# Two MLP-and-pooling layers on one core: the first pair of hidden tiles reordered by tiles of x, its weights and their halves sent and used in another order

## What is computed

```python
h = gelu(x @ fc1_w.T + fc1_b)                 # 512 -> 2048, exact gelu
y = concat(h @ fc2_w.T + fc2_b,               # 2048 -> 384, shared
           h @ experts_w[tok].T + experts_b[tok])   # 2048 -> 128, one expert per sequence
x = x + y
s = tanh(x @ W1 + b1) @ v                     # one score per row
p = softmax(where(mask[type], s[None, :], -1e30))   # per row: prefix, suffix or all but itself
x = x + (p @ x) / mask.sum(-1)
```

## Time and profile before

| | |
|---|---|
| median of 3 runs | 784.71 us (783.61 to 785.57) |
| the profiled execution | 784.57 us |
| its span | 782.8 us |
| TensorE busy | 770.2 us, 98% of the span, 3462 matmuls |
| VectorE busy | 402.5 us, 51% |
| ScalarE busy | 387.0 us, 49% |
| GpSimd busy | 132.7 us, 17% |

### The profile page before, as it was taken

How to read it: one execution, slowest core, us unless ns; L and a number is a source line. 1 busy time by engine, 2 the same in 40 slices (tenths; PEclk the granted TensorE clock), 3 DMA queues, 4 the chain that set the end, 5 groups by cost and what they waited for, 6 DMA issues and landing times.

```text
span 782.8 us, 11478 instructions
## 1 busy us (share of the span) xinstructions
PE 770.2 (98%) x3462; PEld 626.9 (80%) x3462; DVE 402.5 (51%) x713; ACT 387.0 (49%) x665; POOL 132.7 (17%) x184
## 2 busy tenths in 40 slices
PE   9999999999999999999999999999999999999977
PEld 6788888888888888888888888888887888888865
DVE  6854667563445332754536433376245542255666
ACT  6856665443546433543546633446254653344552
POOL 3172221400011121410001022050001102114011
PEclk9999999999999999999999999999999999999998
DMA  6899998877854568867776466985787466787722
GB/s 215 281 346 330 307 338 271 268 228 231 236 190 149 175 204 280 259 202 239 225 228 188 147 209 216 284 253 178 232 252 219 144 194 207 223 284 208 228 67 108
DMA packets 130715, 176.93 MB, mean 226 GB/s; under 512 B 10064, under 2 KB 97632, under 8 KB 130656
## 3 DMA queue, kind: packets, MB, share of 16 engines
q1 hardware_dynamic: 130496, 176.20, 72.0%
q0 software_dynamic: 160, 0.01, 0.0%
HBM read 136.33 MB, written 39.85 MB: 225 GB/s over the span
## 4 chain that ended last, share of the span: by engine, by line
PE 95%; DVE 2%; ACT 1%; DMA 1%; issue 0%; SPq 0%; DVEq 0%; ACTq 0%
PE y L765 15%; PE y L767 15%; PE y L766 15%; PE hA L765 8%; PE hA L767 7%; PE hA L766 7%; PE hF L765 6%; PE hF L766 6%; PE hF L767 5%; PE j L858 2%; PE j L765 1%; PE j L767 1%; PE j L766 1%; PE j L866 1%; PE j L835 1%; PE j L834 1%
## 5 line engine op out<-in xcount | busy, mean ns | idle before, releaser
L765 PE MATMUL y<-hs,w2c 128*128 128x512 f32 x512 | 201.8, 394 | 0.2
L767 PE MATMUL y<-hs,w2c 128*128 128x512 f32 x512 | 199.6, 390 | 0.0
L766 PE MATMUL y<-hs,w2c 128*128 128x512 f32 x512 | 199.4, 389 | 0.0
L765 PEld LDWEIGHTS y<-hs,w2c 128*128 128x128 f32 x512 | 96.1, 188 | 22.1 <-DVE hs L1263 1.9
L767 PEld LDWEIGHTS y<-hs,w2c 128*128 128x128 f32 x512 | 96.1, 188 | 20.5
L766 PEld LDWEIGHTS y<-hs,w2c 128*128 128x128 f32 x512 | 96.2, 188 | 19.3
L765 PE MATMUL hA<-xch,w1c 128*128 128x512 f32 x252 | 100.0, 397 | 0.9 <-DVE xcl L1263 0.6
L767 PE MATMUL hA<-xch,w1c 128*128 128x512 f32 x252 | 98.6, 391 | 0.0
L766 PE MATMUL hA<-xcl,w1c 128*128 128x512 f32 x252 | 98.6, 391 | 0.0
L1035 ACT ACTIVATE hst<-hst,bcol 128x512 f32<-128x512 f32 x62 | 43.9, 721 | 85.3 <-DVE hst L1458 85.3
L1263 DVE TENSOR_TENSOR hs<-gb,hs 128x512 fp32r<-128x512 f32 x64 | 43.5, 716 | 65.1 <-ACT hs L981 65.1
(11 more groups left out here) (283 smaller groups left out, 1096.3 us busy)
## 6 DMA issues: line engine op xcount, KB each, us to landing
w2c<-w2s SPq DMA_DIRECT2D x114, 384.0 KB, 3.5
w1c<-w1s SPq DMA_DIRECT2D x24, 768.0 KB, 4.6
w2c<-exs SPq DMA_DIRECT2D x114, 128.0 KB, 4.0
w1c<-w1s SPq DMA_DIRECT2D x48, 256.0 KB, 3.5
w1c<-w1s SPq DMA_DIRECT2D x24, 512.0 KB, 4.1
x1T<-in_x SPq DMA_DIRECT2D x32, 256.0 KB, 5.6
w1s<-w1c SPq DMA_DIRECT2D x8, 768.0 KB, 4.4
w2s<-w2c SPq DMA_DIRECT2D x16, 384.0 KB, 4.5
```

Of the source, the lines that this page charges most:

```text
L765: nc.tensor.matmul(ps, ah, bh, start=first, stop=False, skip_group_check=onto)
L766: nc.tensor.matmul(ps, ah, bl, start=False, stop=False, skip_group_check=onto)
L767: return nc.tensor.matmul(ps, al, bh, start=False, stop=last, skip_group_check=onto)
```

## The change

- TensorE takes the eight plain products in twos that share a block of x. For each tile of x it runs both weights' high part by the high part of x, with their low parts, and only then both weights by the low part of x. Each matmul now waits only for the half that it reads (`w1hi`, `w1lo`, `xhi`, `xlo`) instead of the first of three waiting for all.
- One matmul on zeros less ahead of it (`WARM` 8 to 7).
- SP sends weight tile `A11` by itself and first, then the first tile of x, then `A21` by itself: one DMA more, every later load of the head one issue later.
- ACT and DVE split `A11` ahead of the first tile of x, `A22` ahead of the second tile of `B21`, and `split_w1(1, 0)` ahead of `B22`. On DVE the two `sum_head(T1, k)` move back, behind `B21`.

```diff
--- before.py
+++ after.py
@@ -63,12 +63,13 @@
 
 A21, B12 = S3, T1
 PLAIN = [(A11, B11, 0), (A21, B11, 1), (A11, B12, 2), (A21, B12, 3), (A12, B21, 0), (A22, B21, 1), (A12, B22, 2), (A22, B22, 3)]
+
 PLAIN_W = [A11, A21, A12, A22]
 
 
 
 UNITS = 2 * HC
-WARM, FILLS = 8, 6
+WARM, FILLS = 7, 6
 W2R = 4
 HSR = 3
 
@@ -299,7 +300,7 @@
         w1sum = sem("w1sum")
         W1hi, W1lo = sem("W1hi"), sem("W1lo")
         xsum, hsum, xhi, xlo, xnhi = sem("xsum"), sem("hsum"), sem("xhi"), sem("xlo"), sem("xnhi")
-        b12hi, b12lo, plain_in = sem("b12hi"), sem("b12lo"), sem("plain_in")
+        b12hi, b12lo, plain_in = sem("b12hi"), sem("b12lo"), [sem(f"plain_in{i}") for i in range(2)]
         ysum, x1hi, x1lo = sem("ysum"), sem("x1hi"), sem("x1lo")
         chain = sem("chain")
         exp_done = sem("exp_done")
@@ -587,10 +588,15 @@
 
             def load_plain(m):
 
-                sp.dma_start(w1raw[0][:, m:m + 3:2, :], fc1_w[:, 0:2, m * W:(m + 1) * W]).then_inc(w1raw_in[0] if m else plain_in, 16)
-
+                sp.dma_start(w1raw[0][:, m:m + 3:2, :], fc1_w[:, 0:2, m * W:(m + 1) * W]).then_inc(w1raw_in[0], 16)
+
+            def load_first(w, row):
+
+                sp.dma_start(w1raw[0][:, w, :], fc1_w[:, row, 0:W]).then_inc(plain_in[row], 16)
+
+            load_first(A11, 0)
             load_x_head(0, 0)
-            load_plain(0)
+            load_first(A21, 1)
             load_x_head(0, 1)
             load_x_head(1, 0)
             load_x_head(1, 1)
@@ -792,18 +798,28 @@
                 last.then_inc(fc1_done, 1)
 
             def plain_pair():
-                for i, (w, x_, m) in enumerate(PLAIN):
-                    pe.wait_ge(w1lo, PLAIN_W.index(w) + 1)
+                for i in range(0, len(PLAIN), 2):
+                    x_ = PLAIN[i][1]
                     for k in range(KH):
+                        cols = slice(k * P, (k + 1) * P)
+                        xh, xl = (b12h[:, k, :], b12l[:, k, :]) if x_ == B12 else (xch[:, x_, k, :], xcl[:, x_, k, :])
+                        if x_ == B12:
+                            pe.wait_ge(b12hi, k + 1)
+                        else:
+                            pe.wait_ge(xhi, HEAD_SPLITS.index((x_, k)) + 1)
+                        for w, _, m in PLAIN[i:i + 2]:
+                            pe.wait_ge(w1hi, PLAIN_W.index(w) + 1)
+                            nc.tensor.matmul(hp[m][:, :], w1c[:, w, 0, cols], xh, start=i < 4 and k == 0, stop=False)
+                            pe.wait_ge(w1lo, PLAIN_W.index(w) + 1)
+                            nc.tensor.matmul(hp[m][:, :], w1c[:, w, 1, cols], xh, start=False, stop=False)
                         if x_ == B12:
                             pe.wait_ge(b12lo, k + 1)
                         else:
                             pe.wait_ge(xlo, HEAD_SPLITS.index((x_, k)) + 1)
-                        xh, xl = (b12h[:, k, :], b12l[:, k, :]) if x_ == B12 else (xch[:, x_, k, :], xcl[:, x_, k, :])
-                        cols = slice(k * P, (k + 1) * P)
-                        last = three(hp[m][:, :], w1c[:, w, 0, cols], w1c[:, w, 1, cols], xh, xl, i < 4 and k == 0, i >= 4 and k == KH - 1)
-                    if i > 0:
-                        last.then_inc(fc1_done, 1)
+                        for j, (w, _, m) in enumerate(PLAIN[i:i + 2]):
+                            last = nc.tensor.matmul(hp[m][:, :], w1c[:, w, 0, cols], xl, start=False, stop=i >= 4 and k == KH - 1)
+                            if k == KH - 1 and i + j > 0:
+                                last.then_inc(fc1_done, 1)
 
             def fc2(kind, b, n, oc):
 
@@ -996,7 +1012,10 @@
                 hi(w1c[:, lo_:hi_, 0, :], raw).then_inc(w1hi, 1)
 
             def split_plain(w):
-                act.wait_ge(plain_in if w in (A11, A21) else w1raw_in[0], 16)
+                if w in (A11, A21):
+                    act.wait_ge(plain_in[0 if w == A11 else 1], 16)
+                else:
+                    act.wait_ge(w1raw_in[0], 16)
                 hi(w1c[:, w, 0, :], w1raw[0][:, w, :]).then_inc(w1hi, 1)
 
             def split_w2(n):
@@ -1231,21 +1250,21 @@
                 act.wait_ge(landed[1], 16)
                 hi(b12h[:, k, :], src[1]).then_inc(b12hi, 1)
 
+            split_plain(A11)
             split_head(B11, 0)
-            split_plain(A11)
+            split_plain(A21)
             split_head(B11, 1)
-            split_plain(A21)
             split_b12(0)
             split_b12(1)
             split_plain(A12)
             split_head(B21, 0)
+            split_plain(A22)
             split_head(B21, 1)
-            split_plain(A22)
+            split_w1(1, 0)
             split_head(B22, 0)
             split_head(B22, 1)
             split_head(T1, 0)
             split_head(T1, 1)
-            split_w1(1, 0)
             split_w1(1, 1)
             act.wait_ge(bias_in, 16)
             gelu_plain(0)
@@ -1552,24 +1571,24 @@
                 wait(dve, hsum, HEAD_SUMS.index(x_) * KH + k)
                 nc.vector.tensor_tensor(src[to], src[a], src[c], ALU.subtract).then_inc(hsum, 1)
 
+            split_plain(A11)
             split_head(B11, 0)
-            split_plain(A11)
+            split_plain(A21)
             split_head(B11, 1)
-            split_plain(A21)
             split_b12(0)
             split_b12(1)
+            split_plain(A12)
+            split_head(B21, 0)
+            split_plain(A22)
+            split_head(B21, 1)
             sum_head(T1, 0)
             sum_head(T1, 1)
-            split_plain(A12)
-            split_head(B21, 0)
-            split_head(B21, 1)
-            split_plain(A22)
+            split_w1(1, 0)
             split_head(B22, 0)
             split_head(B22, 1)
             sum_w1(1)
             split_head(T1, 0)
             split_head(T1, 1)
-            split_w1(1, 0)
             split_w1(1, 1)
             sum_head(T2, 0)
             sum_head(T2, 1)
```

## The result

The changed kernel takes 786.60 us (median of 22 executions, 784.28 to 788.35), the kernel before 784.06 us (22 executions, 783.14 to 785.57). The ratio is 1.0026, with a 95% interval of 1.0018 to 1.0035. The medians lie 2.5 us apart and the means 2.1 us (786.22 and 784.15), to the slower side, where 784.2 and a small gain had been forecast. The profiled execution took 786.58 us.

What follows compares the result with a forecast made beforehand. TensorE, busy 770.2 of 782.8 us, was taken as the bound, with the end riding on `P1`'s start. That start 0.55 earlier, less 0.08 for a pause, gave 784.57 - 0.47 = 784.10, as a median 784.2; range 782.9 to 785.7 us.

Steps and rivals of the forecast that it cites:

- The start of the head: First real matmul on TensorE at 4.80, upper end 5.02, 0.61 us earlier, with no pause from there on.
- The clock's rise: TensorE's clock goes from 1.2 to 2.4 GHz at 8.37, 3.57 us after 4.80, against 10.84 before.
- Same rise: Rival, chance 0.22: clock rises at 10.84 again, S is 19.60, execution 0.43 us longer, median 785.1 us.
- bound (a): Lower bound for S: 6.48 us after the 23rd matmul's end, for which `split_w1(1, 0)` waits; 18.45 or 19.60.
- Bound (b): Lower bound for S from DVE's queue of sums and low parts ahead of the first gelu: 18.70, whatever the clock.
- S: Start of `P1` on TensorE, behind the first pair: forecast 18.70 against 19.25 before, 0.55 us earlier.
- the pause was priced at 0.08 us: TensorE's pause before `P1` was to cost only a slower first matmul, 0.08 us.
- forecast of -0.47: Whole execution 0.47 us shorter: 0.55 gained at S less 0.08 for the pause.
- Splits don't bind: Rival, chance 0.13: S is TensorE's own 17.44, 1.81 us gained, median 782.9 us.
- More waits: Rival, chance 0.07: waits cost 0.03 to 0.05 us on each of 48 first-pair matmuls; median 785.2 to 785.9 us.
- The gain that was forecast: S 0.55 us earlier, as the later of bound (a) and Bound (b), where TensorE alone would gain 1.81.

Runs made afterwards that it cites:

- number 2: Changed kernel with 11 matmuls on zeros added between the first pair and `P1`; ratio to the kernel before 1.0020.
- number 12: Changed kernel with 7 matmuls on zeros added between the first pair and `P1`; ratio to the kernel before 1.0005.
- number 8: Changed kernel with 8 matmuls on zeros at the start instead of 7; ratio to the kernel before 1.0021.
- number 1: Changed kernel with the list moves of `A22`, `split_w1(1, 0)` and, on DVE, the two `sum_head(T1, k)` taken back; ratio to the kernel before 1.0003.
- number 3: Kernel before with only the new order and waits of the first pair's 48 matmuls; ratio to the kernel before 1.0009.
- number 11: Kernel before with only `sum_w1(1)` moved ahead of the low parts of `B22` on DVE; ratio to the kernel before 0.9997.
- number 6: Changed kernel with only `split_w1(1, 0)` put back behind `T1` on ACT and DVE; ratio to the kernel before 1.0017.
- number 7: Kernel of number 1 with `sum_w1(1)` moved from DVE to GpSimd, ahead of its index loads; ratio to the kernel before 0.9998.
- 10: Kernel of number 1 with `sum_w1(1)` moved ahead of the low parts of `B22` on DVE; ratio to the kernel before 0.9989.
- 5: Changed kernel with only DVE's two `sum_head(T1, k)` put back ahead of `A12`; ratio to the kernel before 1.0013.
- number 9: Kernel before with only the new loads (`A11` alone and first, `A21` by itself) and first splits; ratio to the kernel before 1.0011.

## Why the prediction was wrong

**The start of the head: right, with some luck.** 4.80 was forecast and 4.76 measured, with no pause before the seventh matmul. In the eight other traces with the same head and seven zeros the first real matmul lies at 4.70 to 5.47, in four of them behind the forecast's upper end of 5.02. In number 2 `A21` was late as well (a wait of 0.62 us before 6.44).

**The clock's rise: earlier than forecast.** 8.37 was taken and 6.18 measured. I had carried over 3.57 us from the end of the last pause; the rise came 1.42 us after the first real matmul. "Same rise", the rival, didn't happen in this trace. That the place varies from execution to execution, as the Trainium skill's "TensorE: Matmul & The Clock Gate" has it (part 1, the HAM clock gate), is borne out: the changed kernel and number 12 are the same program up to the 48th matmul, and the rise is at 6.18 in one trace and 9.42 in the other; numbers 8 and 1, with the same loads and matmul order, have it at 6.29 and 7.52. In number 12, with the rise at 9.42, ACT did wait for the 23rd matmul, and bound (a) taken from that matmul gives 19.26, so the mechanism of "same rise" holds where the clock is late.

**Bound (b), DVE's queue: the right mechanism, 0.6 us short.** Forecast for the sums of `T1` 11.45 and 12.27, for `split_w1(1, 0)` 12.88, for the two tiles of `B22` 13.21 and 13.82, and S = 18.70. Measured: 12.07, 12.89, 13.50, 13.83, 14.43, and 19.35. The five are 0.61 or 0.62 late and S 0.65, because `B21` was split from 9.80 and 10.80 on, where I took 9.3 and 10.17. I had allowed for 9.65 and no more. That was the wrong size for the added load, and not bad luck: with the old loads ACT gets that tile at 9.19, 9.25 and 9.31 (before, numbers 3 and 11), with the new ones at 9.56 to 10.89 in eleven traces, ten of them behind 9.65. Bound (a) didn't bind: ACT waited at 12.10 for the raw weights and not for the 23rd matmul. The working had said that none of the raw weights is waited for; here that cost nothing, since DVE was busy up to 13.50. (By its own terms bound (a) gives t = 13.10 and 11.94 where the working has 13.12 and 11.97; nothing hangs on it.)

**The step that failed: the pause was priced at 0.08 us.** The prediction had TensorE ready at 17.44 and S at 18.70, a pause of 1.3 us, and charged it with the slower first matmul alone. In the trace both ends moved apart, TensorE's to 16.51 and S to 19.35, 2.84 us, and behind that pause the clock fell. The stretch up to the copy of `P5` took 1.70 us more, where the 0.08 stood: with S 0.65 us later than forecast and 0.2 in the rest of the kernel that makes up the 2.5 us between the forecast of -0.47 and the measured 2.0. The fall is in two traces, this one and number 8, and number 2, with the pause filled and `P1` even later, has none. The mean clocks agree, as far as they tell: half of the changed kernel's executions, 2.1 us slower than the others, have the lower one; with the pause shortened (number 1) or filled (numbers 2 and 12) such executions are 0 of 11, 1 of 12 and 0 of 11. And number 12 gets 0.2% back by zeros alone. All this accounts for about half of the mean loss; what makes up the other half stays open. The working had given a pause and stopped there; what TensorE's clock does in it was asked for the head's start only.

**The rivals.** "Splits don't bind" is refuted by the pause itself. "Same rise" has the right sign, but its late rise didn't happen in the profiled execution, and its loss of 0.43 us is far too small. "More waits" is refuted by the spacing of 0.23 in the changed trace and in number 3. The mechanism that came true is not among them: a head that is faster on TensorE and no faster on DVE, and a pause between the two in which the clock falls.

**The gain that was forecast** hung on S getting earlier by the smaller of two margins. Loads, matmul order and first splits without the list moves (number 1) are level with before (1.0003). I read that as the later tiles taking what the early start gives, since in the traces of the changed kernel and number 1 `P1` waits for the gelu, which hangs on DVE and on landings and not on TensorE; no run separates the two.

What stays open: the half of the loss that no fall of the clock explains; how the loss splits between the three list moves (two of them taken back alone give 1.0013 and 1.0017, overlapping, the third was never tried alone); and which pause brings the clock down. Its length alone doesn't tell: from the last matmul's start to `P1` it is 2.6 us in number 6 (16.72 to 19.33) without a fall, and in number 7 the clock fell at 15.56 behind a start-to-start distance of 2.26 (11.81 to 14.07), in number 3 at 8.94 behind one of 2.15 (5.46 to 7.61).

## What to carry to other kernels

When a change makes the busiest engine finish a stage sooner, work out when the last condition of the next stage comes, too; if that doesn't move, the gain is a pause, and on TensorE a pause can cost the clock for microseconds behind it (about 1.6 us here, in two traces). Before a list of splits is reordered, look in the trace for the idle times of the engine that walks it: the two sums stood in a gap in which DVE waited for data, and the move put them into the full part of its queue. That these two sums are what hurt is read from the rows; by time alone the three moves weren't told apart. Zeros in a pause are a cheap test of such a theory, and a load added at the head of a queue is paid for by the tiles behind it. And where one execution's clock rises 3 us after another's, a single trace shows a mechanism but not its share of the median.

## What the runs showed of the hardware

- The clock fell behind a pause of 2.67 us and rose again 3 us later (19.96 to 22.95), in number 8 behind one of 2.65 us (20.02 to 23.40), in number 7 behind one of 1.87 us and in number 3 behind one of 1.67 us; it stayed up over the pauses before `P1` of numbers 1, 10, 5 and 6, which are 0.95, 1.22, 1.50 and 2.23 us long.
- The same program up to the 48th matmul had its clock rise at 6.18 in one execution and at 9.42 in another. In the other traces it lies anywhere from before 5.99 (number 11, where the matmuls are 0.23 apart from there on) to 14.35 (number 9).
- GpSimd's operations on 128x256 f32 (0.72 to 1.07 us each) about double DVE's beside them: 0.68 to 1.22 us for 128x512, 0.42 to 0.94 for 128x256. The Trainium skill's "GPSIMD Engine Reference" says in section 1, Specifications, that GpSimd shares SBUF interfaces with VectorE and contends with DVE instructions that have two SBUF inputs; the trace agrees, and has the price.
- Landing times of the same loads differ between executions by up to a microsecond: the raw weights of the second pair came at 12.10, 12.23, 12.59 and 13.06 in four traces with the same list of loads, as ACT's waits for them show.
